# Expert slots of a hybrid transformer kernel: the pass over the rounding remainder stands third in both products

## The reference, cut to what matters

```python
logits = jnp.einsum('th,eh->te', x, gate_w)
probs = jax.nn.softmax(logits, axis=-1)
topw, sel = jax.lax.top_k(probs, TOP_K)              # TOP_K = 2 of E = 8
...
gate_up = jnp.einsum('th,eoh->eto', x, w1)           # w1: (8, 704, 512)
g, u = jnp.split(gate_up, 2, axis=-1)
act = jax.nn.silu(g) * u                             # 352 columns
expert_out = jnp.einsum('eti,ehi->eth', act, w2)     # w2: (8, 512, 352)
out = jnp.einsum('eth,te->th', expert_out, combine)
```

## Time and profile before

| what | us |
|---|---|
| median of three runs | 1755.57 |
| lowest and highest | 1754.47, 1755.64 |
| the profiled execution: its own time | 1758.76 |
| its span, first to last instruction | 1756.5 |
| slots of the first expert block, in the span | 477.3 to 775.8 |
| slots of the second expert block | 1455.5 to 1745.9 |

### The profile page before, as it was taken

How to read it: one execution, slowest core, us unless ns; L and a number is a source line. 1 busy time by engine, 2 the same in 40 slices (tenths; PEclk the granted TensorE clock), 3 DMA queues, 4 the chain that set the end, 5 groups by cost and what they waited for, 6 DMA issues and landing times. The chain is left out here.

```text
span 1756.5 us, 35608 instructions
## 1 busy us (share of the span) xinstructions
PE 1524.9 (87%) x11778; PEld 1248.2 (71%) x11794; DVE 901.2 (51%) x2062; ACT 716.4 (41%) x1777; POOL 635.8 (36%) x625
## 2 busy tenths in 40 slices
PE   3999999997497999955999989998999857999996
PEld 3787778876396889945767667666776447888995
DVE  3677677774521222217677675875867552222221
ACT  2666666664031222224544454543455202222221
POOL 5556555653032435422232222322223202343542
PEclk9999999998698999987999999998999968999998
DMA  5255445544489785432000101001000136987543
GB/s 199 96 189 195 147 165 187 198 152 150 150 268 343 203 246 93 77 49 71 13 31 19 49 20 32 31 20 38 31 19 19 38 114 219 302 238 211 91 79 43
DMA packets 92316, 212.38 MB, mean 121 GB/s; under 512 B 6944, under 2 KB 6944, under 8 KB 90656
## 3 DMA queue, kind: packets, MB, share of 16 engines
q1 hardware_dynamic: 74576, 166.58, 27.0%
q0 software_dynamic: 17472, 40.90, 12.0%
q10 hardware_dynamic: 144, 3.15, 0.5%
HBM read 136.94 MB, written 73.66 MB: 120 GB/s over the span
## 5 line engine op out<-in xcount | busy, mean ns | idle before, releaser
L1243 PE MATMUL bank<-ring,halves 128*128 x1872 | 336.2, 329 | 7.0 <-DVE halves L1199 7.0
L1243 PEld LDWEIGHTS bank<-ring,halves 128*128 128x128 f32 x1872 | 306.9, 191 | 14.7 <-issue 8.2
L493 POOL TENSOR_TENSOR arena<-arena 128x1024 f32<-128x1024 f32 x64 | 123.8, 1934 | 146.3 <-DVE arena L569 144.6
L1624 DVE SCALAR_TENSOR_TENSOR arena<-arena 128x256 f32<-128x256 f32 x240 | 139.8, 625 | 13.1 <-ACT arena L1840 10.3
L1154 ACT ACTIVATE arena<-bank 128x512 f32<-128x512 f32 x78 | 46.7, 598 | 234.6 <-DMA mid_rows<-arena 83.9
L1509 POOL TENSOR_TENSOR arena<-arena 128x1024 f32<-128x1024 f32 x16 | 31.5, 1968 | 274.5 <-ACT arena L1891 247.1
L689 ACT ACTIVATE arena<-arena 128x256 f32<-128x256 f32 x256 | 126.4, 499 | 1.1 <-DVE arena L561 1.1
L768 PE MATMUL bank<-arena 128*128 128x128 f32 x1024 | 124.4, 281 | 1.7 <-ACT arena L670 0.8
L768 PEld LDWEIGHTS bank<-arena 128*128 128x128 f32 x1024 | 118.4, 194 | 7.6 <-issue 2.6
L2097 PE MATMUL bank<-arena 128*128 128x512 f32 x256 | 116.3, 608 | 1.2 <-ACT arena L1884 1.2
L1144 ACT ACTIVATE halves<-bank 128x512 fp32r<-128x512 f32 x78 | 46.6, 597 | 162.4 <-PE bank L1228 162.4
(11 more groups left out here) (261 smaller groups left out, 3288.6 us busy)
## 6 DMA issues: line engine op xcount, KB each, us to landing
ring<-expert_halves SPq DMA_DIRECT2D x16, 4352.0 KB, 18.4
expert_halves<-expert_high SPq DMA_DIRECT2D x16, 1088.0 KB, 8.5
expert_halves<-expert_rest SPq DMA_DIRECT2D x16, 1088.0 KB, 10.9
arena<-in_w_dram SPq DMA_DIRECT2D x8, 1088.0 KB, 7.0
normalised_rows<-arena SPq DMA_DIRECT2D x33, 256.0 KB, 2.0
arena<-in_x_dram SPq DMA_DIRECT2D x32, 256.0 KB, 2.8
arena<-mid_rows SPq DMA_DIRECT2D x32, 256.0 KB, 2.7
w_in_raw<-in_in_w_dram SPq DMA_DIRECT2D x1, 4640.0 KB, 16.4
```

The lines of the kernel that those rows point to most:

```text
L493: nc.gpsimd.tensor_tensor(held, held, spread(rinv[:, HG * g:HG * g + HG], 2, 2 * P), ALU.mult)\
L1243: last = nc.tensor.matmul(bank[1 + 2 * par + part][:, 0:INTER], rows_parts[a][:, par, k * P:k * P + P], weights(at, b, (2 * k + part) * IN ...
L1624: last = nc.vector.scalar_tensor_tensor(out=slot[:, j], in0=cin[:, c, k:k + PAIR], scalar=taps[:, c, k:k + 1], in1=slot[:, j], op0=ALU.mul ...
```

## The change

A second tuple `REST_LAST` is used in `up` and `down`: high by high, high by rest, and then rest by high. `up(s, 0)` waits for `rows_high` ahead of its first pass and for `rows_rest` ahead of its third; `down(s)` does the same with `act_high` and `act_rest`. The other products of the kernel keep `PASSES`. No matmul is added or taken away, and every one has the same operands as before.

```diff
 PASSES = ((0, 0), (1, 0), (0, 1))
+REST_LAST = ((0, 0), (0, 1), (1, 0))
...
                 if part == 0:
-                    pe.wait_ge(rows_rest, s + 1)
+                    pe.wait_ge(rows_high, s + 1)
                     after(pe, act_ready, s - 1)
-                for a, b in PASSES:
+                for a, b in REST_LAST:
+                    if part == 0 and a:
+                        pe.wait_ge(rows_rest, s + 1)
...
                 par = s % 2
-                pe.wait_ge(act_rest, s + 1)
+                pe.wait_ge(act_high, s + 1)
                 after(pe, y_ready, s - 1)
-                for j, (a, b) in enumerate(PASSES):
+                for j, (a, b) in enumerate(REST_LAST):
+                    if a:
+                        pe.wait_ge(act_rest, s + 1)
```

More of the change, by code:

```diff
@@ L1245, in up @@
                                                 weights(at, b, (2 * k + part) * INTER, INTER),
-                                                start=((a, b, k) == (0, 0, 0)), stop=((a, b) == PASSES[-1] and k == KD - 1))
+                                                start=((a, b, k) == (0, 0, 0)), stop=((a, b) == REST_LAST[-1] and k == KD - 1))
                 last.then_inc(up_made if part else gate_made, 1)
@@ L1273, in down @@
                                                 weights(at, b, W1E + k * D, D)[0:n],
-                                                start=((a, b, k) == (0, 0, 0)), stop=((a, b) == PASSES[-1] and k == KI - 1))
+                                                start=((a, b, k) == (0, 0, 0)), stop=((a, b) == REST_LAST[-1] and k == KI - 1))
                     pass_done(j)
```

## The result

The changed kernel takes 1752.74 us (median of 20 runs, of which one, at over twice the time, is left out of the comparison), the kernel before 1755.19: a ratio of 0.9984, 95% interval 0.9976 to 0.9992. It is a little faster, by 0.16% (the medians lie 2.45 us apart), which is inside what the prediction called no change. Forecast was 1760.5, slower, with 1754.3 as the lower end. A second comparison gave 0.9994 (0.9980 to 1.0008). The profiled executions differ by more: spans of 1756.5 before and 1747.5 after.

The account below looks back on a forecast made before the run. Bound by the first gather, then the chain of adds' transfers, then TensorE from the last late gather on. 5.75 - 0.6 - 0.2 = +4.95 us on the median 1755.57 gave 1760.5; range of 8 in 10, 1754.3 to 1763.5.

Parts of the forecast that it names:

- What bounds the kernel: In an expert block: first gather and slots 0 and 1, then the chain of adds' transfers, then TensorE to the end.
- Part 1: Slot 0's first product in both blocks: look-ups end after the rest is ready, so the earlier start gains 0.
- Part 2: Slot 1's first product can start earlier: 0.3 of 0.7 us gained in each block, 0.6 in all.
- Part 3: `down` at the last late gather, idle 0.18 us after `turn`: 0.1 gained per block, 0.2 in all.
- Part 4: Register operations moved between `down`'s look-ups: second pass 0.11 us later, slot 0.25 us longer, 23 late slots, 5.75 us.
- Part 5: The additional wait in each of the two products is already satisfied when TensorE comes: 0.
- The rule of the Trainium skill: With queue depth 64, look-ups run over a slot ahead, third stretch costs nothing; idle 0.20 and 0.26 us speaks against it.
- The look-ups stay hidden: Sequencer far enough ahead, moved register operations cost nothing, gains stay: 1754.8, or 1753.8 with the whole 0.7 twice; chance 0.2.
- 1762.8 and 6 more: Slots with quick look-ups lose their cover too: 1762.8; late slots of the middle stretch also counting: 1768; chance 0.15.
- signs of being wrong: Last gather to end keeps its length, number of long look-ups changes, or adds' chain moves over 1 us for other reasons.

Follow-up runs that it names:

- the order alone: The changed kernel's pass order, with all waits on the rest ahead of the first pass as before: 1762.78 against 1755.50 us, ratio 1.0049.
- the kernel with early look-ups: The kernel before, with both look-ups of each slot moved to between `turn` and `down`'s wait: 1753.97 us (0.9993), and again 1755.67 (1.0007).

## Why the prediction was wrong, point by point

- *What bounds the kernel*: right. Transfers in the middle, TensorE behind them.
- *Part 1, slot 0's rest, 0*: right. The look-ups ahead of the first product end after the rest; the first product starts 6.7 and 6.5 us after the gather's issue in both kernels.
- *Part 2, slot 1's rest, 0.3 of 0.7*: right. It measured 0.3 by the idle times (1.60 less 0.88 and 0.40) and 0.4 by the start of slot 0's `down`.
- *Part 3, "In the third stretch `down` starts without a wait"*: this is the step that failed. The engine had no idle time there, but its sequencer did wait, for the same rest whose wait was being moved; the trace had it, since the first register operation of `down` came when DVE's subtraction ended (1686.3 and 1686.28). The 1.1 us between the second look-up and the third pass, which the prediction read as how far the sequencer gets, was set by how long before its use the rest was ready. The part's 0.2 us at the last late gather wasn't there either: in slot 20 of the second block the idle time in front of `down` fell from 0.18 to 0.05 us, but the next two passes waited 0.59 + 0.38 us, where they had waited 0.39 + 0.32.
- *Part 4, the price*: right, and for another kernel. The 0.11 and 0.25 us per late slot are what the order alone costs. The sentence that didn't hold is that the look-ups "sit at the same place between the end of one `down` and the next": by the change's own wait they moved 0.6 us ahead. The prediction put 23 late slots at 0.25 us more each. Among slots 22 to 36 the trace of before has 22 late ones, and the changed kernel none (one pass came 0.03 late). Slots 20 and 21, at the last late gathers, stayed late: a sequencer that has just waited for a gather has no lead to win.
- *Part 5, waits cost nothing*: nothing in the runs speaks against it. The late stretch at 94.18 us for 14 slots, 6.73 each, holds the two new waits.
- *The rule of the Trainium skill.* The trace of before had a look-up five matmuls ahead of the array; in the kernel with early look-ups the first look-up starts 2.45 us ahead of its slot's `down`, with 12 matmuls and 4 transposes between. So the sequencer's lead is set by the waits in its way, and the prediction was wrong to set the idle time against the rule. The Trainium skill's depth of 64 ("TensorE: Matmul & The Clock Gate", section "Architectural detail: the array is 16× 32×32, not 1× 128×128") isn't contradicted by a lead of 16, and no run here shows it.
- *The rivals.* "The look-ups stay hidden", 1754.8, chance 0.2, comes nearest, but not by the way it named, a sequencer already far enough ahead. It left out that the late slots which exist before would go as well: 0.8 + 1.4 us. Two of the prediction's sums are off by little: the whole 0.7 twice, with the 0.2 of part 3, makes 1754.0 and not 1753.8, and 1762.8 and 6 more make 1768.8 and not 1768.
- *Sign and range.* The predicted +4.95 was 5.75 of part 4 less 0.8. With part 4 at -2.2, part 2 at -0.8 and part 3 at nothing, the sum is -3.0; measured -2.45. One of the prediction's own signs of being wrong came: the long first look-ups, 10 at the end of the second block, went to none. The range ended at 1754.3 because no case took anything from the late slots' present cost.

## What to carry to other kernels

A wait can cost without idle time on its engine: what stands behind it in the sequencer (look-ups, register work) is pushed towards the array, and can show up later as "issue" in front of a matmul. Before pricing work between two matmuls, find when the sequencer reaches it, and what released it: the first register operation behind a wait, beside the end of what it waits for, tells that. Moving the wait to where the data is used gave the lead back; moving the look-ups ahead of the wait cured the same late passes, but put them behind another wait, the one for the gather.

## What the runs showed of the hardware that I had not expected

A register load from SBUF by TensorE's sequencer takes 0.30 us here. At the ends of both blocks it takes 0.73 to 1.03 when the packets of POOL's indirect DMA start within 0.13 us of it (before); started 0.4 to 0.55 us behind the first packets it takes 0.58 to 0.74 (changed). Delaying the transfer by 0.7 us moved the long duration from the first of two loads to the second, in ten slots of ten. What in the transfer holds the load wasn't tried.
